# A conditioned two-layer block on one core: the weight deltas' last batch, their loads and their matmuls in another order

## Chip, core and metric

One core of a Trainium2 chip runs the kernel. Its five engines are TensorE (PE: matmuls and transposes; PEld: its weight loads), VectorE (DVE), ScalarE (ACT), GpSimd (POOL) and SyncE (SP, which here issues every DMA). Each works through its own instructions in program order and waits on semaphores for the others. The metric is the device time of one execution in microseconds (us); lower is better. It is given as the median of several runs; one further execution was taken with the profiler.

## What is computed

`x` is 4 batches x 1024 rows x 512, `cond` is 4 x 128 (one row a batch). Two layers follow each other; all is float32 at the interface.

```python
# layer 0
scale = cond @ norm_w.T + 1.0
h = x * (scale[:, None, :] * rsqrt(mean(x * x) + 1e-6))
val, gate = split(h @ up_w.T)                # up_w: 4096 x 512
h = val * gelu(gate)                         # 2048 wide
hq, wq = act_quant(h), weight_quant(down_w)  # 8 bit by row; -1, 0, 1
x = hq @ wq.T + x
# layer 1: its weights depend on the batch
Wd_b = Wd + ((cond @ Wdd.T + bdd) * 0.1).reshape(B, 128, 512)   # Wdd: 65536 x 128
Wu_b = Wu + ((cond @ Wdu.T + bdu) * 0.1).reshape(B, 512, 128)   # Wdu: 65536 x 128
out = x + relu(x @ Wd_b.T + bd) @ Wu_b.T + bu
```

`Wdd` and `Wdu` hold 32 MB each and are read once; every one of their 65536 rows is multiplied with the four rows of `cond`. These products, the *deltas*, are what the change is about.

## The kernel before

**Chunks and slots.** The 4096 rows of x are cut into 8 chunks of 512 (`c` = 0 to 7), and the 2048 columns of h into 16 tiles. Layer 0 runs chunk after chunk, and in each chunk slot after slot (`j` = 0 to 15, one tile a slot); I write (c, j) for a slot. Every engine's program is `chunks(run)`, a loop over the same chunks and slots, so the order of each engine's work is written out by hand. No common clock keeps the engines at the same slot; only semaphores do.

**A slot.** TensorE computes the gate product (12 matmuls of 512 columns, lines 1173 to 1175), ScalarE its gelu (line 693), TensorE the value product (12 more), VectorE the h product of the two (line 1010), ScalarE its absolute value (line 707), VectorE the running maximum (line 902). In the first eight slots of a chunk VectorE and ScalarE also quantise the chunk before (lines 875, 668, 671). In slots 9 to 12 TensorE adds a down product (16 matmuls, line 1277) for 128 rows of the chunk before at the end of the slot; VectorE adds the x rows to it in the slot after (the residual, line 965), and SP stores them and loads the next x rows.

**Deltas on TensorE.** Wdd and half of Wdu are cut into 96 *units* of 128 x 1024 words, each loaded as two halves (`load_nat`, line 382; three buffers `nat`). VectorE turns the two halves of a unit (`turn_nat`, line 892) into `natT`, which has room for four units. Four units make a *batch* (24 batches, m = 0 to 23): `delta_products(m)` (line 1232, 32 small matmuls) waits until all eight halves of the batch are turned and writes into the PSUM bank HY. After every second batch ScalarE copies the bank into `stage` (`read_sums`) and SP stores that to DRAM (`store_stage`).

**The unit table.** `unit_slots` says which units VectorE turns in which slot: one in an ordinary slot, two in slots 9 to 12, none in the slot after a batch's last unit. `batch_at(c, j)` is the batch whose last unit was turned in the slot before (c, j). With this table the 24 delta products stand in the slots (1,1), (1,6), (1,10), (1,13), (2,2), (2,7), (2,11), (2,15), (3,4), (3,9), (3,12), (4,1), (4,6), (4,10), (4,13), (5,2), (5,7), (5,11), (5,15), (6,4), (6,9), (6,12), (7,1) and (7,6).

**Deltas on GpSimd.** The other half of Wdu is cut into 64 *parts*. SP loads a part (`load_part`, line 404), GpSimd multiplies and adds (`multiply_part`, lines 561 to 568), VectorE sums the rest (`sum_part`, line 906). `sum_slots` and `load_slots` say in which slots. A part may only be loaded when GpSimd is nearly through with the part two before it.

**The deltas come back.** In the last chunk, at slot 6, `load_deltas` issues 32 loads from the DRAM scratch into `delta_d` and `delta_u` (the place of `natT`). At slots 10 to 13 TensorE turns one batch of x a slot (`turn_delta_down`, line 1244, and `turn_delta_up`, line 1251), and VectorE adds them to the weights a slot later (`layer_of_batch`). `turn_delta_down(b)` for b > 0 waits for VectorE's work on batch b - 1 of x. After the last chunk comes layer 1, which the change doesn't touch.

**SP's order in a slot** (`run` of SP, line 439 on): x of the next chunk and its turns, weight rows of the units (each waits for the turn of the unit whose buffer it takes), parts, x rows for the residual (`load_xr`, line 409) and their stores, `store_stage`, and at (7,6) `load_deltas`. Everything behind an instruction that waits is issued later too.

TensorE's order in a slot of a later chunk is:

```python
pe.wait_ge(gelu_done, n - 1)
up_products(par, FT + j, GATE[j % 2], gate_full)
...
for m in batch_at(c, j):
    delta_products(m)
if last and 10 <= j < 14:
    turn_delta_down(j - 10)
...
up_products(par, j, VAL[j % 2], val_full)
```

Of the kernel before, what the change touches and what calls it, by code (L numbers as in the profile page):

```python
# [25 lines left out]
def conditioned_block(nc, x, cond, norm_w, up_w, down_w, Wd, bd, Wu, bu, Wdd, bdd, Wdu, bdu, out):  # L26
# [27 lines left out]
    with ExitStack() as ctx:  # L54
# [134 lines left out]
        def first_bank(c, k):  # L189
# [38 lines left out]
        delta_back, delta_turned, layers_ready, layers_hi, layers_split = (sem(n) for n in (  # L228
            "delta_back", "delta_turned", "layers_ready", "layers_hi", "layers_split"))
# [68 lines left out]
        unit_slots, free_from = {}, 13  # L298
        for n in range(FT * NCH):
            long_slot = n >= FT and 9 <= n % FT < 13  # L300
            while free_from <= n and sum(map(len, unit_slots.values())) < UNITS and len(unit_slots.get(n, [])) < 1 + long_slot:
                u = sum(map(len, unit_slots.values()))
                unit_slots.setdefault(n, []).append(u)
                if u % NATT == NATT - 1:
                    free_from = n + 2
# [7 lines left out]
        def batch_of(m):  # L313
# [4 lines left out]
                     for j in ((7, 9, 10, 11, 12, 13, 15) if c == 1 else (1, 3, 5, 7, 8, 9, 10) if c == NCH - 1 else (1, 3, 5, 7, 9, 10, 11, 12, 13, 15))]  # L318
        load_slots = [FT + 3, FT + 3, FT + 6] + [n + 1 for n in sum_slots[:PARTS - 3]]
# [11 lines left out]
        def _(sp):  # L331
# [56 lines left out]
            def load_deltas():  # L388
                sp.wait_ge(stage_free, 16 * (GROUPS + 1))
                sp.wait_ge(nat_turned, 2 * UNITS)  # L390
                for b in range(NB):
                    for k in range(2):
                        n0 = 64 * k
                        sp.dma_start(delta_d[n0:n0 + 32, b, :], delta_of[0][0, b, :, k, 0:4, :]).then_inc(delta_back, 16)
                        for y in range(2):
                            n1 = n0 + 32 + 16 * y
                            sp.dma_start(delta_d[n1:n1 + 16, b, :], delta_of[1][y, b, :, k, 0:4, :]).then_inc(delta_back, 16)
                        sp.dma_start(delta_u[:, 2 * k, b, :], delta_of[0][1, b, :, k, 0:4, :]).then_inc(delta_back, 16)
# [40 lines left out]
            def run(c, par, b):  # L439
                first, last = is_first(c), b is None  # L440
                for j in range(FT):
# [31 lines left out]
                    if c == 1 and j == 3:  # L473
                        sp.wait_ge(piece_quant, FT)
# [9 lines left out]
                    for m in batch_at(c, j):  # L484
                        if m % 2 == 1:
                            store_stage(m)
                    if last and j == 6:
                        load_deltas()
                        sp.wait_ge(x_scaled, TT * NCH - 1)
                        sp.dma_start(bu_bc[:, :], bu.rearrange("(a d) -> a d", a=1).to_broadcast([P, D])).then_inc(bu_in, 16)  # L490
# [48 lines left out]
        def _(pool):  # L539
# [31 lines left out]
            def run(c, par, b):  # L571
# [5 lines left out]
                for i in range(PARTS):  # L577
                    slot = sum_slots[max(i - 2, 0)]
                    if slot // FT == c:
                        if not normed and (i == 1 if c == 1 else slot % FT >= 6):  # L580
                            norm_x(c + 1)
                            normed = True
                        multiply_part(i)
# [554 lines left out]
        def _(pe):  # L1138
# [97 lines left out]
            def turn_delta_down(b):  # L1236
                if b == 0:
                    pe.wait_ge(delta_back, 16 * NB * 8)
# [52 lines left out]
            def run(c, par, b):  # L1291
# [7 lines left out]
                for j in range(FT):  # L1299
# [4 lines left out]
                    if first:  # L1304
                        pe.wait_ge(w_lo_done, halves_done(j, 0))
                    if not (first and j < 2):
                        pe.wait_ge(gelu_done, n - 1)
# [3 lines left out]
                    for m in batch_at(c, j):  # L1311
                        delta_products(m)
# [206 lines left out]
```

## Time and profile before

| | us |
|---|---|
| Median of 3 runs | 947.32 |
| Lowest and highest | 946.69, 947.43 |
| The profiled execution | 946.8 |
| Its span, first to last instruction | 944.6 |
| TensorE busy | 924.6 |
| VectorE busy | 682.3 |
| GpSimd busy | 640.6 |
| ScalarE busy | 428.3 |
| Mean granted clock of TensorE | 0.996 |

The 2.2 us between the profiled execution's time and its span lie outside the first and the last instruction. All times of rows are counted from the start of the span. A timeline row gives start, duration, engine, line of the kernel, operation, output and input; where the engine stood idle before it, the idle time and what ended it stand in brackets. TensorE's matmuls are pipelined: a matmul of 512 columns is shown as 0.38 us long while the next begins 0.22 us after it, so slots are measured from start to start. Chunk c's slots are found in the timeline by the h products of VectorE (line 1010), of which there is one a slot.

### The profile page before, as it was taken

Reading aid. Unit: us, or ns where it says so; the run is one execution under the profiler, and the core shown is the slowest. Engines: PE = TensorE matmul, PEld = TensorE weight load, DVE = VectorE, ACT = ScalarE, POOL = GpSimd, SP = SyncE. Lnnn points to the kernel's source line nnn. Section 1 sums busy time; section 2 is a strip of 40 time slices with the busy share of each in tenths; the row PEclk is TensorE's granted clock in tenths of the full one; section 3 lists DMA queues with packets and bytes.
Section 4 is the critical chain, followed back from the end, with each engine's and each line's share of the span. In section 5 each row is a group of like instructions: output and inputs, shape, how many; then the busy total and the mean of one; then the engine's idle time right before and its main releaser. Section 6 shows DMA issues by size and latency. Waiting matters only on the chain. (4 is left out here: it accounts for less than half of the span.)

```text
span 944.6 us, 13871 instructions
## 1 busy us (share of the span) xinstructions
PE 924.6 (98%) x5002; PEld 454.2 (48%) x5002; DVE 682.3 (72%) x1034; ACT 428.3 (45%) x788; POOL 640.6 (68%) x565
## 2 busy tenths in 40 slices
PE   9999999999999999999999999999999999599998
PEld 6555544444444444444444444444444444245586
DVE  6778877877877588767878687777877694156666
ACT  7898676224731276225632275224722264014343
POOL 1000009989987999799987899799988997300664
PEclk9999999999999999999999999999999999989999
DMA  8799644565255454564355553563446451221584
GB/s 293 240 218 216 171 140 130 142 191 164 82 151 157 127 168 130 142 162 136 111 157 161 129 166 111 153 184 111 124 131 185 131 179 56 79 67 35 189 301 178
DMA packets 142059, 144.04 MB, mean 152 GB/s; under 512 B 51876, under 2 KB 89256, under 8 KB 141480
## 3 DMA queue, kind: packets, MB, share of 16 engines
q1 hardware_dynamic: 141992, 143.17, 52.0%
q8 instruction: 39, 0.64, 0.3%
q14 instruction: 28, 0.23, 0.1%
HBM read 112.46 MB, written 19.92 MB: 140 GB/s over the span
## 5 line engine op out<-in xcount | busy, mean ns | idle before, releaser
L561 POOL TENSOR_TENSOR delta_reg<-delta_reg,s_bc 128x512 f32<-128x512 f32 x256 | 327.2, 1299 | 153.3 <-DMA delta_reg<-in_L_cond_Wdu 141.9
L1173 PE MATMUL bank<-x_split,w_hi 128*128 128x512 f16 x1016 | 386.5, 380 | 0.0
L1174 PE MATMUL bank<-x_split,w_hi 128*128 128x512 f16 x1016 | 386.1, 380 | 0.0
L1175 PE MATMUL bank<-x_split,w_lo 128*128 128x512 f16 x1016 | 386.1, 380 | 0.0
L892 DVE STREAM_TRANSPOSE delta_reg<-delta_reg 128x512 f32<-128x512 f32 x192 | 198.7, 1117 | 17.6 <-DMA delta_reg<-in_L_cond_Wdd 13.9
L707 ACT ACTIVATE bank<-h 128x512 f32<-128x512 f32 x126 | 75.7, 601 | 292.7 <-DVE h L1010 292.5
L1010 DVE SCALAR_TENSOR_TENSOR h<-bank,desc,g 128x512 f32<-128x512 f32 x128 | 95.2, 743 | 110.5 <-issue 89.3
L564 POOL TENSOR_TENSOR delta_reg<-delta_reg 128x512 f32<-128x512 f32 x128 | 166.9, 1304 | 10.0
L1173 PEld LDWEIGHTS bank<-x_split,w_hi 128*128 128x128 f16 x1016 | 99.6, 98 | 122.1 <-issue 10.7
L1175 PEld LDWEIGHTS bank<-x_split,w_lo 128*128 128x128 f16 x1016 | 99.6, 98 | 120.5 <-issue 1.1
L1174 PEld LDWEIGHTS bank<-x_split,w_hi 128*128 128x128 f16 x1016 | 99.6, 98 | 112.7 <-issue 0.8
L693 ACT ACTIVATE g<-bank,desc 128x512 f32<-128x512 f32 x128 | 87.3, 682 | 115.1 <-PE bank L1175 114.9
L568 POOL TENSOR_TENSOR delta_reg<-delta_reg 128x256 f32<-128x256 f32 x128 | 96.0, 750 | 12.9 <-DVE delta_reg L906 3.1
L1277 PE MATMUL bank<-wqT,qreg 128*128 128x512 fp8e4 x448 | 101.3, 379 | 1.4 <-DVE xr L965 1.4
L902 DVE TENSOR_TENSOR absrun<-bank,absrun 128x512 f32<-128x512 f32 x118 | 81.2, 688 | 21.4 <-ACT bank L707 21.4
L668 ACT ACTIVATE h<-h 128x512 f32<-128x512 f32 x112 | 64.7, 623 | 36.6 <-DVE h L875 36.6
L875 DVE TENSOR_TENSOR h<-h,bank 128x512 f32<-128x512 f32 x112 | 71.6, 683 | 0.0
L1277 PEld LDWEIGHTS bank<-wqT,qreg 128*128 128x128 bf16 x448 | 43.7, 98 | 53.8 <-DVE xr L965 1.6
L671 ACT ACTIVATE qreg<-h 128x512 bf16<-128x512 f32 x112 | 63.6, 616 | 0.0
L965 DVE SCALAR_TENSOR_TENSOR xr<-bank,fy,xr 128x512 f32<-128x512 f32 x30 | 22.3, 745 | 40.4 <-issue 19.1
L604 POOL TENSOR_TENSOR out_own<-xn,sc_row 128x512 f32<-128x512 f32 x8 | 10.1, 1287 | 58.9 <-DVE h L1117 56.3
L906 DVE TENSOR_REDUCE delta_reg<-delta_reg 128x16 f32<-128x512 f32 x64 | 41.8, 652 | 10.2 <-POOL delta_reg L568 10.2
(182 smaller groups left out, 754.7 us busy)
## 6 DMA issues: line engine op xcount, KB each, us to landing
delta_reg<-in_L_cond_Wdd SPq DMA_DIRECT2D x128, 256.0 KB, 2.9
delta_reg<-in_L_cond_Wdu SPq DMA_DIRECT2D x128, 256.0 KB, 3.2
qreg<-in_L_cond_up_w SPq DMA_DIRECT2D x32, 256.0 KB, 4.4
xr<-in_x SPq DMA_DIRECT2D x30, 256.0 KB, 3.9
x_scratch<-xr SPq DMA_DIRECT2D x30, 256.0 KB, 3.5
xn<-in_x SPq DMA_DIRECT2D x7, 1024.0 KB, 7.5
h<-in_L_cond_down_w SPq DMA_DIRECT2D x4, 1024.0 KB, 6.8
delta_reg<-in_L_cond_down_w SPq DMA_DIRECT2D x8, 512.0 KB, 4.6
```

The lines of the kernel that those rows point to most:

```text
L561: pool.tensor_tensor(part_mul[:, b, :, :], part_w[:, i % 2, :, :], cond_all[:, 2 * pair + b, :].unsqueeze(1).to_broadcast([P, 4, C]), ALU. ...
L564: pool.tensor_tensor(part_mul[:, :, :, 0:64], part_mul[:, :, :, 0:64], part_mul[:, :, :, 64:128], ALU.add).then_inc(part_step, 1)
L568: pool.tensor_tensor(part_low[:, i % 2, 2 * pair:2 * pair + 2, :, :], part_mul[:, :, :, 0:32], part_mul[:, :, :, 32:64], ALU.add).then_inc ...
L693: act.activation(g[:, j % 2, :], GATE[j % 2][:, :], ACT.Gelu, scale=desc[:, 2 * j + 1:2 * j + 2]).then_inc(gelu_done, 1)
L707: act.activation(abs_tile(c, j), h[:, j, :], ACT.Abs).then_inc(abs_done, 1)
L892: dve.transpose(natT[:, t, k, :, :].rearrange("p a (r e) -> p e a r", e=4), nat[:, v % HALVES, :]).then_inc(nat_turned, 1)
L902: dve.tensor_tensor(absrun[:, :], abs_tile(c, j), absrun[:, :], ALU.max).then_inc(max_done, 1)
L1010: dve.scalar_tensor_tensor(h[:, j, :], VAL[j % 2][:, :], desc[:, 2 * j:2 * j + 1], g[:, j % 2, :], ALU.mult, ALU.mult).then_inc(h_done, 1)
L1173: pe.matmul(bank[:, :], w_hi[:, k, cols], xh[:, par, k, :], start=(k == 0), stop=False)
L1174: pe.matmul(bank[:, :], w_hi[:, k, cols], xl[:, par, k, :], start=False, stop=False)
L1175: mm = pe.matmul(bank[:, :], w_lo[:, k, cols], xh[:, par, k, :], start=False, stop=(k == KD - 1))
L1277: mm = pe.matmul(Y[:, :], q[:, f, t * P:(t + 1) * P], wqT[:, f, :], start=(f == 0), stop=(f == FT - 1))
```

## The change

It has four parts.

1. The unit table is built in another way. After a batch's last unit the next slot now turns one unit fewer than usual (none in an ordinary slot, one in slots 9 to 12), where it turned none before in either. From chunk 3 on every chunk has the same pattern. The 24 delta products now stand in the slots (1,1), (1,6), (1,10), (1,13), (2,2), (2,7), (2,11), (2,14), and then 3, 8, 11 and 14 of chunks 3, 4, 5 and 6. None is left in chunk 7.
2. GpSimd's parts are loaded and summed sooner: the first three loads two slots sooner, the sums of chunk 1 begin at slot 5 and not 7, one sum fewer stands in chunk 7, and a part's load stands in a slot of a sum and not in the slot after it. GpSimd's `norm_x(2)` now comes before part 3, where it came before part 1.
3. `load_deltas` loads one batch of x a call, at slots 1 to 4 of chunk 7, and has a semaphore for each batch of x; `turn_delta_down(b)` waits for its own.
4. TensorE's `delta_products` stands ahead of the gate product of its slot and not behind it.

```diff
-        unit_slots, free_from = {}, 13
-        for n in range(FT * NCH):
+        unit_slots, units, batch_end = {}, 0, -1
+        for n in range(FT - 3, FT * NCH):
             long_slot = n >= FT and 9 <= n % FT < 13
-            while free_from <= n and sum(map(len, unit_slots.values())) < UNITS and len(unit_slots.get(n, [])) < 1 + long_slot:
-                u = sum(map(len, unit_slots.values()))
-                unit_slots.setdefault(n, []).append(u)
-                if u % NATT == NATT - 1:
-                    free_from = n + 2
+            for _ in range(1 + long_slot - (batch_end == n - 1)):
+                if units < UNITS and batch_end != n:
+                    unit_slots.setdefault(n, []).append(units)
+                    units += 1
+                    if units % NATT == 0:
+                        batch_end = n
...
-                     for j in ((7, 9, 10, 11, 12, 13, 15) if c == 1 else (1, 3, 5, 7, 8, 9, 10) if c == NCH - 1 else (1, 3, 5, 7, 9, 10, 11, 12, 13, 15))]
-        load_slots = [FT + 3, FT + 3, FT + 6] + [n + 1 for n in sum_slots[:PARTS - 3]]
+                     for j in ((5, 7, 9, 10, 11, 12, 13, 15) if c == 1 else (1, 3, 5, 7, 9, 10) if c == NCH - 1 else (1, 3, 5, 7, 9, 10, 11, 12, 13, 15))]
+        load_slots = [FT + 1, FT + 1, FT + 4] + sum_slots[:PARTS - 3]
...
-            def load_deltas():
-                sp.wait_ge(stage_free, 16 * (GROUPS + 1))
-                sp.wait_ge(nat_turned, 2 * UNITS)
-                for b in range(NB):
-                    for k in range(2):
...
+            def load_deltas(b):
+                if b == 0:
+                    sp.wait_ge(stage_free, 16 * (GROUPS + 1))
+                    sp.wait_ge(nat_turned, 2 * UNITS)
+                for k in range(2):
...
-                    if c == 1 and j == 3:
-                        sp.wait_ge(piece_quant, FT)
+                    if c == 1 and j == 1:
+                        sp.wait_ge(piece_quant, FT - 2)
...
+                    if last and 1 <= j <= NB:
+                        load_deltas(j - 1)
                     if last and j == 6:
-                        load_deltas()
...
-                        if not normed and (i == 1 if c == 1 else slot % FT >= 6):
+                        if not normed and slot % FT >= 6:
...
             def turn_delta_down(b):
+                pe.wait_ge(delta_back[b], 16 * 8)
                 if b == 0:
-                    pe.wait_ge(delta_back, 16 * NB * 8)
...
+                    for m in batch_at(c, j):
+                        delta_products(m)
                     if not (first and j < 2):
                         pe.wait_ge(gelu_done, n - 1)
                     up_products(par, FT + j, GATE[j % 2], gate_full)
                     if not first and j == 0:
                         turn_absrun(c - 1)
-                    for m in batch_at(c, j):
-                        delta_products(m)
```

## Rows read from the trace of the kernel before

**Rows 1.** The page: busy time of the engines; granted clock in 40 slices.
```profile
PE 924.6 (98%) x5002; PEld 454.2 (48%) x5002; DVE 682.3 (72%) x1034; ACT 428.3 (45%) x788; POOL 640.6 (68%) x565
...
PEclk9999999999999999999999999999999999989999
```

**Rows 2.** Waits of PE: line, releaser: total us, times, longest.
```profile
PE bank L1232 <- DVE delta_reg L892: 1.9, 3, 0.6
```

**Rows 3.** Timeline of PE, chunk 7: start, us, engine, line, operation [idle <-releaser].
```profile
804.49 0.38 PE L1173 MATMUL bank<-x_split,w_hi 128*128 128x512 f16 x1
...
809.50 0.66 PE L1244 MATMUL bank<-identf,delta_reg 128*128 128x128 f32 x4 [2.26 <-DMA delta_reg<-delta_scratch]
...
814.38 3.63 PE L1277 MATMUL bank<-wqT,qreg 128*128 128x512 fp8e4 x16 [1.41 <-DVE xr L965]
...
827.70 1.12 PE L1244 MATMUL bank<-identf,delta_reg 128*128 128x128 f32 x4 [7.11 <-DVE wd_first L921]
...
836.97 0.38 PE L1173 MATMUL bank<-x_split,w_hi 128*128 128x512 f16 x1
...
846.25 0.38 PE L1173 MATMUL bank<-x_split,w_hi 128*128 128x512 f16 x1
...
852.09 0.38 PE L1173 MATMUL bank<-x_split,w_hi 128*128 128x512 f16 x1
```

**Rows 4.** Timeline of SP's queue, chunk 7.
```profile
789.73 0.34 SPq L394 DMA_DIRECT2D delta_reg<-delta_scratch  x1
...
808.47 0.43 SPq L409 DMA_DIRECT2D xr<-in_x  x1
```

**Rows 5.** Timeline of DVE, chunk 7, slot 10.
```profile
813.57 0.75 DVE L965 SCALAR_TENSOR_TENSOR xr<-bank,fy,xr 128x512 f32<-128x512 f32 x1 [10.17 <-DMA xr<-in_x]
823.69 0.69 DVE L906 TENSOR_REDUCE delta_reg<-delta_reg 128x16 f32<-128x512 f32 x1 [9.37 <-POOL delta_reg L568]
```

**Rows 6.** Timeline of PE, early slots of chunks 1, 2 and 3.
```profile
117.50 0.38 PE L1173 MATMUL bank<-x_split,w_hi 128*128 128x512 f16 x1
...
120.89 1.93 PE L1232 MATMUL bank<-delta_reg,cond_diag 128*32 128x256 f32 x32 [0.64 <-DVE delta_reg L892]
...
229.97 0.38 PE L1173 MATMUL bank<-x_split,w_hi 128*128 128x512 f16 x1
...
233.32 1.93 PE L1232 MATMUL bank<-delta_reg,cond_diag 128*32 128x256 f32 x32 [0.60 <-DVE delta_reg L892]
...
336.09 0.38 PE L1173 MATMUL bank<-x_split,w_hi 128*128 128x512 f16 x1
...
341.27 0.38 PE L1173 MATMUL bank<-x_split,w_hi 128*128 128x512 f16 x1
```

**Rows 7.** Timeline of DVE, chunks 2, 3 and 5.
```profile
233.66 0.73 DVE L1010 SCALAR_TENSOR_TENSOR h<-bank,desc,g 128x512 f32<-128x512 f32 x1
...
257.52 2.07 DVE L892 STREAM_TRANSPOSE delta_reg<-delta_reg 128x512 f32<-128x512 f32 x2
...
312.43 2.06 DVE L892 STREAM_TRANSPOSE delta_reg<-delta_reg 128x512 f32<-128x512 f32 x2
...
339.28 0.78 DVE L1010 SCALAR_TENSOR_TENSOR h<-bank,desc,g 128x512 f32<-128x512 f32 x1
...
341.73 2.10 DVE L892 STREAM_TRANSPOSE delta_reg<-delta_reg 128x512 f32<-128x512 f32 x2
343.64 0.70 DVE L1010 SCALAR_TENSOR_TENSOR h<-bank,desc,g 128x512 f32<-128x512 f32 x1
...
627.26 2.06 DVE L892 STREAM_TRANSPOSE delta_reg<-delta_reg 128x512 f32<-128x512 f32 x2
```

**Rows 8.** Timeline of PE, starts of slots (2,7), (2,14) and (5,14).
```profile
258.51 0.38 PE L1173 MATMUL bank<-x_split,w_hi 128*128 128x512 f16 x1
...
312.53 0.38 PE L1173 MATMUL bank<-x_split,w_hi 128*128 128x512 f16 x1
...
628.51 0.38 PE L1173 MATMUL bank<-x_split,w_hi 128*128 128x512 f16 x1
```

More of the change, by code:

```diff
@@ L227, in conditioned_block @@
             "nat_turned", "delta_mm", "stage_full", "stage_free"))
-        delta_back, delta_turned, layers_ready, layers_hi, layers_split = (sem(n) for n in (
-            "delta_back", "delta_turned", "layers_ready", "layers_hi", "layers_split"))
+        delta_back = [sem(f"delta_back{b}") for b in range(NB)]
+        delta_turned, layers_ready, layers_hi, layers_split = (sem(n) for n in (
+            "delta_turned", "layers_ready", "layers_hi", "layers_split"))
         xr_in = [sem(f"xr_in{i}") for i in range(2)]
@@ L386, in store_stage @@
                 sp.dma_start(delta_dram[m // 2, :, :], stage[:, :]).then_inc(stage_free, 16)
-            def load_deltas():
-                sp.wait_ge(stage_free, 16 * (GROUPS + 1))
-                sp.wait_ge(nat_turned, 2 * UNITS)
-                for b in range(NB):
-                    for k in range(2):
[L393 to L398, printed above, removed]
+            def load_deltas(b):
[3 more added lines that the diff above has]
+                for k in range(2):
+                    n0 = 64 * k
+                    sp.dma_start(delta_d[n0:n0 + 32, b, :], delta_of[0][0, b, :, k, 0:4, :]).then_inc(delta_back[b], 16)
+                    for y in range(2):
+                        n1 = n0 + 32 + 16 * y
+                        sp.dma_start(delta_d[n1:n1 + 16, b, :], delta_of[1][y, b, :, k, 0:4, :]).then_inc(delta_back[b], 16)
+                    sp.dma_start(delta_u[:, 2 * k, b, :], delta_of[0][1, b, :, k, 0:4, :]).then_inc(delta_back[b], 16)
             def load_part(i):
```

## The prediction

> **What bounds the kernel now.** I read the page first. TensorE is busy for 924.6 of 944.6 us, the others for at most 682.3 [rows 1], so only two things can move the time: an interval in which TensorE stands idle or runs at the lower clock, and work added to it. The change adds none; it moves work. The question is therefore where TensorE waits, and where it will wait.
>
> The timeline of TensorE has one bad place, the last chunk's slots 10 and 11: it waits 2.26, 1.41 and 7.11 us [rows 3], 10.8 us together. The clock digits are 9 in every slice but one, and that slice (826 to 850 us) begins within the 7.11 us stall [rows 1]. The chain behind it is read on the issuing queue. SP issues the 32 loads of the summed deltas in one piece (and bu's behind them), from 789.73 until the x rows' own at 808.47 [rows 4]: 18.7 us in which the x rows, and Wdu part 63 right behind them, stand in the queue. VectorE then waits 10.17 us for the x rows and 9.37 us for GpSimd's sums of part 63, and gets to them at 823.69 [rows 5]; TensorE's 7.11 us is the end of that chain.
>
> Everywhere else in chunks 1 to 7 TensorE waits three times, for 1.9 us together, for VectorE's transposes ahead of a delta product [rows 2]. They are small, but they say that this wait is already tight where the product stands today, behind a gate product.
>
> **The change part by part.**
>
> *Deltas loaded a batch a slot, last batch a chunk sooner.* From the unit table: the last delta product moves from (chunk 7, slot 6) to (6,14), so the stage is stored before chunk 7 and the loads can go at (7,1) to (7,4), eight each. 18.7 us for 32 issues is 4.7 us for eight, against 5.18 us for a plain slot (336.09 to 341.27 [rows 6]), and SP has no weight rows to load there any more. Part 63 is asked for at slot 5 and x rows at slot 7, behind no block of loads. All three stalls lose their cause. The gain is best read as lengths: slot 10's start to slot 14's start took 852.09 − 804.49 = 47.6 us; slots 12 and 13 of the same kind, undisturbed, took 9.28 and 5.84 [rows 3]; three of the first and one of the second are 33.7. **Gain 13.9 us**, of which 10.8 is idle and 3.1 the slow clock and restarts. What is late next there: turning batch b+1's delta waits for VectorE's batch b; in slots 12 and 13 that was already so and cost nothing [rows 3]. The extra per-batch waits on TensorE are met six slots ahead: nothing.
>
> *Parts a slot sooner, GpSimd's first norm behind part 2.* GpSimd is below TensorE in busy time [rows 1] and gets its first part two slots sooner, so it is further ahead. SP's wait for GpSimd at an earlier slot is the risk: the loads queued behind it are x rows and the next weight rows. The norm is wanted at (1,8) and comes about (1,7). I charge nothing; the cover is GpSimd's head start of two slots, some 10 us.
>
> *Delta products ahead of the gate product.* 24 products of the same cost, so no added work. But TensorE runs in order, and `delta_products(m)` waits for the batch's eight transposes, of which the last two are VectorE's in the slot before. Today a gate product (12 matmuls, 2.6 us) lies between; now nothing does. If VectorE is late by the end of a slot, TensorE stands, and nothing later gives it back, as it waits for nothing else in these chunks. Queued behind the wait are gate, value and down products, that is everything. So I take the 24 batches by their new slot and compare the end of the last transposes with the start of that slot.
>
> - (1,1), batch 0. TensorE's slot began at 117.50, the product could begin at 120.89 [rows 6]. It now waits 3.4 us instead of 0.64: 2.75 more.
> - (2,2), batch 4. 229.97 and 233.32 [rows 6], 3.35 instead of 0.60: 2.75 more. The third old wait (0.6, [rows 2], batch 15 at (5,2)) goes, as that batch moves.
> - (3,3), (4,3), (5,3), (6,3). Batches now end in slot 2 of each of these chunks, where VectorE still works off what chunk start piled up. In chunk 3 slot 2's transposes ended at 341.73 + 2.10 = 343.83, TensorE's slot 3 began at 341.27 [rows 6, 7]: 2.6 us. That chunk had no unit in slot 15 before it; the new table has one there, as chunk 2 had. In chunk 2 VectorE's h product (line 1010) of slot 1 came 233.66 − 229.97 = 3.7 us after TensorE's slot 2 start, in chunk 3 it came 339.28 − 336.09 = 3.2 [rows 6, 7]: 0.5 later. So 2.6 to 3.1; I take 3.0, the chunk with the same units in slots 15 to 1: 12.0 us for four.
> - (2,7). Slot 6 holds the mean square: transposes to 257.52 + 2.07 = 259.59, slot 7 from 258.51 [rows 7, 8]: 1.1.
> - (3,8) to (6,8), four. One slot after that; VectorE gains 0.8 a slot (343.64 − 339.28 = 4.4 against 5.18, [rows 6, 7]): 0.25 each, 1.0. Bounds 0 and 1.1 each.
> - (2,14) to (6,14), five. In slot 13 the transposes stand behind the residual of x rows 3, whose load SP issues behind slot 12's four weight loads. With the same units in slots 12 and 13, chunk 2 ended them at 312.43 + 2.06 = 314.49 against a slot 14 start of 312.53, chunk 5 at 629.32 against 628.51 [rows 7, 8]: 2.0 and 0.8. Five at 1.4: 7.0. Bounds: 0, if the x rows land in time, and 2.0 each.
> - The other eight, in (1,6), (1,10), (1,13) and slot 11: a down product of 3.4 us (9.28 − 5.84, [rows 3]) or a TensorE already late by batch 0 lies between: 0.
>
> Sum: 2.75 + 2.75 − 0.6 + 12.0 + 1.1 + 1.0 + 7.0 = **26.0 us lost**, against 13.9 gained: +12.1. The profiled execution took 946.8 us (span 944.6), so 958.9; the median of the runs is 0.5 above it, so **959 us**.
>
> With all lower ends (5.5 − 0.6 + 10.4, nothing at slots 7, 8 and 14): 15.3 lost, +1.4, 948.7. With all upper ends (5.5 − 0.6 + 12.4 + 1.1 + 4.4 + 10.0): 32.8 lost, +18.9, 966.2.
>
> **The rivals.**
>
> *Clock.* The new waits at slot 3, (1,1) and (2,2) are idle gaps of about 3 us, six of them. Gaps of 2.26 and 1.41 left the clock at full, 7.11 was followed by the lower level [rows 1, 3], and 3 lies nearer to the first. If each of the six were followed by a slow stretch like that one's, it would cost up to 3.1 each, 18.6 in all: 978; three of six, 969. For it: it has happened once here. Against: TensorE is fully busy on both sides of each gap. Chance 0.10.
> The Trainium skill, page "TensorE: Matmul & The Clock Gate", section "Why this matters for your kernels", advises to leave no long idle gap between bursts of matmuls, or the clock drops to the lower level. The 7.11 us stall agrees; by that rule read strictly the six gaps make this rival, and by the two short gaps they don't.
>
> *Faster.* Only (1,1), (2,2) and (2,7) cost what I say, and the waits of slots 3 and 14 do not come, because SP's loads leave sooner and VectorE is never behind. Then 5.5 − 0.6 + 1.1 = 6.0 is lost and 946.8 − 13.9 + 6.0 = 939. It decides at 13.9 − 6.0 = 7.9 us for these nine places, 0.9 each: below that the change wins. For it: slot 14's wait hangs on when one load lands, and ranged from 0.8 to 2.0. Against: in slot 2 VectorE's operations follow each other without idle time [rows 7], so no earlier load makes it sooner. Chance 0.13.
>
> *The last chunk isn't cured.* Part 63 or the x rows still come late, because SP now waits for GpSimd at earlier slots and the delta loads queue behind that. Then the 13.9 is not there and the 26.0 is: 973. Against: by its new place part 63 is asked for five slots ahead of its sum. Chance 0.04.
>
> **How the numbers follow.** The forecast's own cases run from 949 to 966 with 0.68, and its low end down to no change with 0.05; the clock has 0.10, no cure 0.04, faster 0.13. Within 0.2% (1.9 us, about what a measurement of this kernel can tell from no change) is 945.4 to 949.2. So slower 0.82, same 0.05, faster 0.13. The range that leaves out the faster case and the upper part of the clock and no-cure cases is 948 to 972.
>
> **What would show it.** In the new trace: SP's delta loads at chunk 7's slots 1 to 4, no stall of TensorE in its slots 10 and 11 and a full clock to the end (the gain); waits of line `delta_products` for VectorE's transposes, in place of 3 of 0.6 us, some 15 with 20 to 27 us in total, the longest near 3 us at the start of slot 3 of chunks 3 to 6 (the loss). I am wrong if those waits total less than 14 us, if they are there but TensorE later finds the time again, or if a clock digit of chunks 1 to 6 falls below 9.

## The result: 3.5% slower, nearly three times as far from before as forecast

| | before | changed |
|---|---|---|
| median of the runs | 947.01 us (946.10 to 947.43, 4 runs) | 980.71 us (977.31 to 982.90, 4 runs) |
| ratio to before | 1 | 1.0354, 95% interval 1.0323 to 1.0385 |
| profiled execution, its span | 946.8, 944.6 us | 982.9, 980.7 us |
| mean granted clock of TensorE | 0.996 | 0.987 |

The forecast was 959 us with a range of 948 to 972; the sign was right, the size was not: 33.7 us slower by the medians where 12 were forecast. The profiled execution is the slowest of the four and has the lowest clock; the other three had 0.991 to 0.993, so what is said of the low clock below is the upper end of what it cost. The page of the changed kernel, busy time and granted clock, to be laid beside [rows 1]:

```profile
PE 933.5 (95%) x5002; PEld 455.6 (46%) x5002; DVE 695.5 (71%) x1034; ACT 429.0 (44%) x788; POOL 645.0 (66%) x565
...
PEclk9999999999999999999899999999999999999999
```

The same 5002 matmuls keep TensorE busy for 8.9 us more; the rows below show where they ran at the lower clock. A digit below 9 now stands in the middle of the kernel (466 to 490 us), not in the last chunk. TensorE's waits (line, releaser: total us, times, longest), against the 1.9 us in 3 of [rows 2]; line 1235 is the delta product, line 895 VectorE's transposes of the weight rows:

```profile
PE bank L1235 <- DVE delta_reg L895: 38.4, 20, 4.0
```

Some 15 waits with 20 to 27 us were forecast. TensorE's timeline shows four of the twenty, and what stands behind some of them:

```profile
267.19 1.93 PE L1235 MATMUL bank<-delta_reg,cond_diag 128*32 128x256 f32 x32 [2.01 <-DVE delta_reg L895]
...
413.80 1.93 PE L1235 MATMUL bank<-delta_reg,cond_diag 128*32 128x256 f32 x32 [0.95 <-DVE delta_reg L895]
...
472.45 3.64 PE L1235 MATMUL bank<-delta_reg,cond_diag 128*32 128x256 f32 x32 [3.97 <-DVE delta_reg L895]
476.02 0.61 PE L1176 MATMUL bank<-x_split,w_hi 128*128 128x512 f16 x1
476.42 0.63 PE L1177 MATMUL bank<-x_split,w_hi 128*128 128x512 f16 x1
...
556.08 3.60 PE L1235 MATMUL bank<-delta_reg,cond_diag 128*32 128x256 f32 x32 [2.01 <-DVE delta_reg L895]
559.62 0.39 PE L1176 MATMUL bank<-x_split,w_hi 128*128 128x512 f16 x1
```

The number behind the start is the duration: the same 32 matmuls take 1.93 us at 267 and 3.6 us at 472 and 556, and at 476 the gate product's matmuls take 0.61 in place of 0.38 us. These are stretches at the lower of the clock's two levels. Beside [rows 3], the last chunk's slots 10 to 14 in TensorE's timeline (a product of line 1176 at each slot's start):

```profile
854.53 0.38 PE L1176 MATMUL bank<-x_split,w_hi 128*128 128x512 f16 x1
...
863.82 0.38 PE L1176 MATMUL bank<-x_split,w_hi 128*128 128x512 f16 x1
...
873.11 0.38 PE L1176 MATMUL bank<-x_split,w_hi 128*128 128x512 f16 x1
...
888.23 0.38 PE L1176 MATMUL bank<-x_split,w_hi 128*128 128x512 f16 x1
```

No stall is left there, slots 10 and 11 take 9.29 us each, and slot 10 to slot 14 takes 33.7 us against 47.6. SP's queue, beside [rows 4], now spreads the loads; part 63 goes out at 824.80 between them and the x rows:

```profile
804.41 0.44 SPq L396 DMA_DIRECT2D delta_reg<-delta_scratch  x1
...
824.80 0.59 SPq L406 DMA_DIRECT2D delta_reg<-in_L_cond_Wdu  x1
825.44 0.50 SPq L493 DMA_DIRECT2D sc_row<-in_L_cond_bu  x1
825.98 0.92 SPq L411 DMA_DIRECT2D xr<-in_x  x2
```

**The balance of the 36.1 us** between the two profiled executions: 38.4 − 1.9 = 36.5 of waits, minus 13.9 in the last chunk, is 22.6. The low clock adds 10.4: a delta product's start to the next gate product's takes 1.87 us at full clock and 3.20, 3.47, 3.04, 3.57, 3.54 and 2.89 behind six of the waits (8.5 us more together), and in three of them the twelve gate matmuls take 2.85, 3.15 and 3.00 in place of 2.38 (1.9 more). That makes 33.0. Of the remaining 3.1, waits of TensorE that the kernel before doesn't have take 1.5 (for the scales `s` 0.7, `absmax` 0.5, x rows 0.3); 1.6 I can't assign to a row.

### The profile page after: what moved, and what is told of

Read it like the earlier page. It is cut to its first block, busy times and chain, and to the rows that moved or that the text cites. A ratio compares the mean times of both kernels' runs of the same rounds, so it can differ in the third digit from the quotient of the medians.

```text
span 980.7 us, 13874 instructions
## 1 busy us (share of the span) xinstructions
PE 933.5 (95%) x5002; PEld 455.6 (46%) x5002; DVE 695.5 (71%) x1034; ACT 429.0 (44%) x788; POOL 645.0 (66%) x565
## 4 chain that ended last, share of the span: by engine, by line
PE 77%; DVE 8%; DMA 5%; issue 3%; POOL 3%; ACT 2%; SPq 1%; DVEq 0%; POOLq 0%; ACTq 0%
PE bank L1176 19%; PE bank L1177 19%; PE bank L1178 19%; PE bank L1280 6%; PE bank L1235 5%; DVE delta_reg L895 4%; DMA delta_reg<-in_L_cond_Wdd 4%; POOL delta_reg L564 1%; PE bank L1290 1%; DVE absrun L905 1%; POOL delta_reg L567 1%; PE bank L1417 1%; PE bank L1426 1%; PE bank L1156 1%; PE bank L1447 1%
## 5 line engine op out<-in xcount | busy, mean ns | idle before, releaser
L564 POOL TENSOR_TENSOR delta_reg<-delta_reg,s_bc 128x512 f32<-128x512 f32 x256 | 331.8, 1317 | 90.7 <-DMA delta_reg<-in_L_cond_Wdu 77.7
L895 DVE STREAM_TRANSPOSE delta_reg<-delta_reg 128x512 f32<-128x512 f32 x192 | 196.7, 1107 | 20.7 <-DMA delta_reg<-in_L_cond_Wdd 17.2
L1176 PEld LDWEIGHTS bank<-x_split,w_hi 128*128 128x128 f16 x1016 | 99.6, 98 | 124.2 <-issue 12.6
L571 POOL TENSOR_TENSOR delta_reg<-delta_reg 128x256 f32<-128x256 f32 x128 | 94.8, 741 | 92.1 <-DVE delta_reg L909 83.6
L1235 PE MATMUL bank<-delta_reg,cond_diag 128*32 128x256 f32 x768 | 54.9, 435 | 38.4 <-DVE delta_reg L895 38.4
L1235 PEld LDWEIGHTS bank<-delta_reg,cond_diag 128*32 128x32 f32 x768 | 24.9, 122 | 66.3 <-DVE delta_reg L895 48.8
```

The lines of the kernel that those rows point to most:

```text
L564: pool.tensor_tensor(part_mul[:, b, :, :], part_w[:, i % 2, :, :], cond_all[:, 2 * pair + b, :].unsqueeze(1).to_broadcast([P, 4, C]), ALU. ...
L571: pool.tensor_tensor(part_low[:, i % 2, 2 * pair:2 * pair + 2, :, :], part_mul[:, :, :, 0:32], part_mul[:, :, :, 32:64], ALU.add).then_inc ...
L895: dve.transpose(natT[:, t, k, :, :].rearrange("p a (r e) -> p e a r", e=4), nat[:, v % HALVES, :]).then_inc(nat_turned, 1)
L1176: pe.matmul(bank[:, :], w_hi[:, k, cols], xh[:, par, k, :], start=(k == 0), stop=False)
L1235: mm = pe.matmul(HY[32 * t:32 * t + 32, cols], cond_diag[:, a, :], natT[:, (4 * m + t) % NATT, :, a, :], start=(a == 0), stop=(a == HB - 1))
```

## The experiments

My theory A: moving the delta products ahead of the gate product costs it all, in waits and in the low clock behind them, and the other parts of the change gain about what the last chunk lost. Rival B: the other parts lose time too. In the table, the waits for transposes are TensorE's in the profiled execution, and the clock is its mean granted clock there. Each run was timed against the kernel before on the same chip: 945.19 us beside the runs e1, e2, e7 and e8, 946.21 beside e3 to e6, 946.24 beside e9, e12 and e13; intervals are of 95%.

| run | median, us | ratio (interval) | waits for transposes | clock |
|---|---|---|---|---|
| e1_behind_gate | 939.21 | 0.9931 (0.9914 to 0.9947) | 4.6 us in 8 | 0.999 |
| e2_order_alone | 973.47 | 1.0296 (1.0281 to 1.0312) | 22.6 in 12 | 0.989 |
| e3_old_parts | 972.98 | 1.0293 (1.0248 to 1.0338) | 31.9 in 18 | 0.984 |
| e4_units_and_loads | 940.08 | 0.9940 (0.9920 to 0.9960) | 4.1 in 7 | 0.999 |
| e5_parts_alone | 936.77 | 0.9904 (0.9888 to 0.9921) | 1.8 in 3 | 1.000 |
| e6_behind_value | 937.48 | 0.9913 (0.9892 to 0.9933) | none | 1.000 |
| e7_filled | 975.62 | 1.0317 (1.0300 to 1.0334) | 21.8 in 19 | 0.995 |
| e8_turn_first | 960.32 | 1.0147 (1.0118 to 1.0176) | 17.6 in 16 | 0.998 |
| e9_value_turn_first | 946.02 | 1.0013 (0.9988 to 1.0039) | none | 0.997 |
| e12_batchwise_loads | 934.84 | 0.9889 (0.9871 to 0.9907) | 3.6 in 4 | 1.000 |
| e13_batchwise_behind_value | 934.50 | 0.9876 (0.9858 to 0.9894) | none | 1.000 |

### The order of the delta products, undone and alone

**e1_behind_gate**, the changed kernel with the product back behind the gate product:

```diff
-                    for m in batch_at(c, j):
-                        delta_products(m)
                     if not (first and j < 2):
                         pe.wait_ge(gelu_done, n - 1)
                     up_products(par, FT + j, GATE[j % 2], gate_full)
                     if not first and j == 0:
                         turn_absrun(c - 1)
+                    for m in batch_at(c, j):
+                        delta_products(m)
```

> The changed kernel with one part undone: TensorE's delta products stand behind the gate product again. Theory A (the loss is TensorE waiting at a slot's start for transposes of the slot before, and the low clock that follows): the gate product's 2.6 us come off each wait, of the changed kernel's 38.4 us in 20 waits some 4 us stay, the slow stretches (10 us) go, the last chunk's gain of 13.9 us stays: 947.0 - 13.9 + 2 = 935 us. Theory B (the loss comes from the denser unit table and the parts' new slots, which make VectorE, GpSimd and SP late wherever the product stands): most of the 33.7 us stays, above 965 us.

**e2_order_alone**, the kernel before with only this move made, the other way round.

> The kernel before with one part of the change alone: TensorE's delta products ahead of the gate product. Theory A: waits of 3.4 us at (1,1), (2,2), (5,2), 1.3 at (4,1), 1.7 and 1.9 at (3,4) and (6,4), some 1 us at (2,7), (5,7), (2,15), 0.7 at (1,13), (4,13) and (7,1), by the ends of the transposes in the trace of before: 19 us more than before's 1.9, and 2 to 5 us of low clock, none of the last chunk's gain: 947.0 + 19 + 4 = 970 us. Theory B: the old table's waits stay small, under 952 us.

Measured 939.21 and 973.47. Together they show that the move is the loss: taking it out of the changed kernel brings 4.2% of the time (1.0354 against 0.9931, some 40 us), putting it alone into the kernel before costs 3.0%, 28.3 us. Of these, the waits for transposes are 20.7 and the low clock 6.2 (by the same reckoning as above, behind four of the waits). The same move costs some 12 us more on the new table and slots, where the transposes come later: it adds 33.8 us of waits to e1's 4.6, and 20.7 to the 1.9 of the kernel before. In e1 the waits of TensorE are these, the first with 4.6 us where the changed kernel has 38.4, and the last chunk's slots 10 to 14 again take 33.7 us:

```profile
PE bank L1235 <- DVE delta_reg L895: 4.6, 8, 1.5
...
PE bank L1176 <- DVE absrun L905: 0.9, 1, 0.9
PE bank L1280 <- DVE xr L968: 0.8, 1, 0.8
```

The second half of theory A, that the other parts gain what the last chunk lost, holds only in part: e1 came out 4 us above what A expected. With 13.9 gained, 6.0 (by the medians) is what is left. Waits that grew by 2.7, 0.9 and 0.8 account for 4.4 of the missing 7.9; the rest is not assigned.

### The other parts of the change, one by one

**e5_parts_alone**, the kernel before with only the parts' new slots, the earlier wait of SP and the norm's new place:

```diff
-((7, 9, 10, 11, 12, 13, 15) if c == 1 else (1, 3, 5, 7, 8, 9, 10) if c == NCH - 1 else ...
-        load_slots = [FT + 3, FT + 3, FT + 6] + [n + 1 for n in sum_slots[:PARTS - 3]]
+((5, 7, 9, 10, 11, 12, 13, 15) if c == 1 else (1, 3, 5, 7, 9, 10) if c == NCH - 1 else ...
+        load_slots = [FT + 1, FT + 1, FT + 4] + sum_slots[:PARTS - 3]
...
-                        if not normed and (i == 1 if c == 1 else slot % FT >= 6):
+                        if not normed and slot % FT >= 6:
```

> The kernel before with the parts' slots and GpSimd's norm changed alone. The prediction charged nothing: 945.2 us as before, within 1.5. Rival 1 (the last chunk's stalls shrink by themselves, as part 63 is asked for ahead of the 32 loads): the second of the two waits of VectorE (9.4 us) goes, TensorE's 7.1 us stall with it, 936 to 940 us. Rival 2 (SP waits for GpSimd ahead of x rows): 947 to 950 us.

Measured 936.77: the first rival. The prediction had charged and credited nothing here. Yet these few numbers take away the 7.11 us stall and its slow clock by themselves. In e5's SP queue part 63 leaves well ahead of the block of delta loads, which still stands in one piece; in TensorE's timeline of the last chunk two small stalls are left of three:

```profile
773.21 0.43 SPq L404 DMA_DIRECT2D delta_reg<-in_L_cond_Wdu  x1
790.76 0.34 SPq L394 DMA_DIRECT2D delta_reg<-delta_scratch  x1
...
809.23 0.91 SPq L409 DMA_DIRECT2D xr<-in_x  x2
```

```profile
810.17 0.66 PE L1244 MATMUL bank<-identf,delta_reg 128*128 128x128 f32 x4 [1.90 <-DMA delta_reg<-delta_scratch]
...
814.20 3.63 PE L1277 MATMUL bank<-wqT,qreg 128*128 128x512 fp8e4 x16 [0.56 <-DVE xr L965]
```

The x rows are loaded no sooner than in [rows 4]. So of the two things that stood behind the block, part 63 was the one that made the long stall.

**e4_units_and_loads**, the kernel before with the new unit table and the loads a batch a slot (parts 1 and 3 of the change), old slots of the parts, product behind the gate product.

> The kernel before with the unit table and the loads of the deltas alone (parts and order of the product as before). Theory A: as the run with the product behind the gate, 939.2 us, since a product behind the gate hides what the parts' slots cost at slot 8; with theory D some of its waits shrink: 937 to 940 us. Rival (the parts' shift is needed for the last chunk's gain): part 63 late again, above 943 us.

Measured 940.08. The two gains don't add up: each change cures the long stall alone (6.1 us faster here, 9.4 in e5), and both together are e1, 6.0 us faster. The unit table brings waits of its own, in e4 in its waits of TensorE for the transposes (4.1 us), the spread of the scales and the residual of the x rows:

```profile
PE bank L1235 <- DVE delta_reg L895: 4.1, 7, 1.5
PE bank L1270 <- DVE s L870: 2.7, 5, 0.8
PE bank L1280 <- DVE xr L968: 2.3, 3, 1.4
```

**e3_old_parts**, the changed kernel with the parts' slots, SP's wait and the norm as before (the diff of e5 turned round).

> The changed kernel with part 2 undone: GpSimd's parts loaded and summed in the slots of the kernel before, the first norm ahead of part 1. Theory D: the parts' new slots lay a GpSimd operation over VectorE's mean-square operation in slot 6 (it takes 1.24 us there, 0.17 us in most chunks of before), and that is why the waits at (2,7) and slot 8 are 2.0 and 0.7 to 1.1 us and not 1.1 and 0.25: they fall by 0.9 us on average, five of them, 980.7 - 4.5 = 976 us. Rival: the waits of these slots are the table's: 980.7 us. Nothing of either says that the 13.9 us of the last chunk go.

Measured 972.98. The interval is wide and overlaps that of the changed kernel (1.0248 to 1.0338, 1.0323 to 1.0385), so the time decides little and the trace has to: the waits for transposes fell from 38.4 to 31.9 us. At slot 8 of chunks 3 to 6 they are 0, 0, 0 and 0.22 in place of 0.71 to 1.11, and at (2,7) 0.95 in place of 2.01, as the prediction had them. At slot 14 they fell too, from 9.8 to 6.0 us over the five; at slot 3 they rose, from 12.6 to 13.9. The reason at slot 8 and (2,7) is in VectorE's timeline in slot 6, where a small operation, the mean square of line 842, lies just ahead of the transposes. The changed kernel, then GpSimd's work at that time, then e3:

```profile
378.90 1.24 DVE L842 TENSOR_SCALAR ss<-ss 128x4 f32<-128x4 f32 x1 [1.31 <-ACT x_split L619]
```

```profile
377.62 2.50 POOL L564 TENSOR_TENSOR delta_reg<-delta_reg,s_bc 128x512 f32<-128x512 f32 x2
```

```profile
379.23 0.17 DVE L842 TENSOR_SCALAR ss<-ss 128x4 f32<-128x4 f32 x1 [1.31 <-ACT x_split L619]
```

It takes 1.24 to 1.27 us in six of the seven times that the changed kernel runs it, and ends with an operation of GpSimd, here the second of two (377.62 + 2.50 = 380.12; 378.90 + 1.24 = 380.14). In e3 it takes 0.17 to 0.45, in the kernel before 0.17 to 0.83 in six of seven. What differs is the moment: in e3 GpSimd's operation is nearly through when the mean square begins, in the changed kernel it has just begun, at most 0.06 us before. GpSimd there waits for VectorE 21 times, 83.6 us in all (3.1 in 3 in the kernel before), and I take this to tie the two to the same place of each chunk:

```profile
POOL delta_reg L571 <- DVE delta_reg L909: 83.6, 21, 7.7
```

The old slots don't keep the two apart by themselves: e4 has them, and its mean square takes 0.58 to 1.06 us in five of seven. e3 undoes all of part 2 at once, so it doesn't tell the parts' slots from SP's wait and the norm.

The Trainium skill, page "SBUF — State Buffer", section "SBUF: two separate sides", says that GpSimd and a VectorE operation of some kinds (in a mode with two ports, or with two inputs in SBUF) hold a shared pair of ports for a whole instruction while the other waits. The ends that coincide agree with it; no run here shows the port itself, or the mode of this operation.

### How late the transposes are, and behind what

**e6_behind_value**, the changed kernel with the product behind the value product, not only behind the gate product:

```diff
                     up_products(par, j, VAL[j % 2], val_full)
+                    for m in batch_at(c, j):
+                        delta_products(m)
```

> The changed kernel with TensorE's delta products at the end of the two products of a slot, behind the value product (5.2 us later than the change has them). Theory A: every wait for transposes is covered (the longest was 4.0 us), so the 5.6 us that the product behind the gate still lost go: 939.2 - 5.6 = 934 us, the fastest of all. Rival (VectorE waits for the product before it may turn the next unit, since four units fill its buffer): the lateness comes back on VectorE in slots 9 and 12, 939 us or more.

Measured 937.48: no wait for a transpose is left. VectorE's lateness is thus nowhere over some 5 us, two products' time. The time is 3.5 us above what was expected. The expected 5.6 us counted 1.0 more than e1 waits for transposes (4.6), and beside e1 the waits for the x rows grew from 0.8 to 2.4 and those for the running maximum from 0.9 to 1.1; 0.7 stays open. The two in e6:

```profile
PE bank L1280 <- DVE xr L968: 2.4, 4, 0.7
...
PE bank L1176 <- DVE absrun L905: 1.1, 1, 1.1
```

**e8_turn_first**, the changed kernel with VectorE's transposes ahead of the quantising and the running maximum in slots 1 to 7. If slot 3's wait is VectorE's queue and not a late load, it must shrink.

```diff
+                    if not first and 0 < j < 8:
+                        turn_units(c, j)
...
-                    if j > 0 and not first:
+                    if j >= 8 and not first:
```

> The changed kernel, and in slots 1 to 7 of every later chunk VectorE turns its units ahead of the quantising and the running maximum, not behind them. Theory A (the waits at slots 3 and 8 are VectorE's own backlog, so its order inside the slot sets them): the last transposes end 1.9 us sooner, waits at (3,3) to (6,3) fall from 3.1 to 1.2 us on average, those at slot 8 and (2,7) go, the clock stays full at slot 3: about -13 us of waits and -5 of slow clock, 962 us. Rival (the weight rows come late, SP's loads set the waits): VectorE would only wait for the rows instead, 978 to 983 us.

Measured 960.32. VectorE's timeline of the changed kernel ahead of slot 3 shows what stood in front, without idle time, and below it is the product in e8, with 0.46 us where 2.88 stood:

```profile
353.66 1.27 DVE L878 TENSOR_TENSOR h<-h,bank 128x512 f32<-128x512 f32 x2
354.85 0.68 DVE L905 TENSOR_TENSOR absrun<-bank,absrun 128x512 f32<-128x512 f32 x1
355.45 2.02 DVE L895 STREAM_TRANSPOSE delta_reg<-delta_reg 128x512 f32<-128x512 f32 x2
```

```profile
351.66 1.93 PE L1237 MATMUL bank<-delta_reg,cond_diag 128*32 128x256 f32 x32 [0.46 <-DVE delta_reg L895]
```

Slot 8's waits went to zero too, and only (1,1), 3.20 us, was still followed by the low clock. But new waits of 4.1 us for the running maximum came: VectorE's order moves the lateness from one result to another.

**e9_value_turn_first**, both: behind the value product, and the transposes first in slots 2 to 7.

> The changed kernel with its delta products behind the value product and with VectorE turning the weight rows ahead of its other work in slots 2 to 7. With the products behind the value product alone TensorE had no wait for transposes left and the time was 937.5 on the same chip as 946.2 for the kernel before. If the time hung on these transposes only, turning them first can bring nothing: 937 to 938. If VectorE's other results (quantised pieces, maxima) come later for it and TensorE waits for them as it did where turning first stood with the product ahead of the gate product (4.1 us in 4 waits there), it is 939 to 942.

Measured 946.02, the median of nine runs (942.48 to 952.97); a tenth took 3446.9 us, which nothing here explains, and is left out. It is worse than both readings: with the transposes no longer awaited, turning them first only delays the rest. In e9 TensorE waits, where e6 had 1.1 and 2.4 us,

```profile
PE bank L1178 <- DVE absrun L905: 7.1, 3, 3.6
PE bank L1282 <- DVE xr L968: 3.1, 5, 1.0
```

### The slow clock behind the gaps

**e7_filled**, the changed kernel with idle matmuls on a free bank ahead of the delta product, 40 of them at (2,2) and at slot 3, 18 at slot 14. They compute nothing that is used.

```diff
+                        if (c, j) == (2, 2) or (c > 1 and j in (3, 14)):
+                            keep_busy({14: 18}.get(j, 40), TA)
                     for m in batch_at(c, j):
                         delta_products(m)
```

> The changed kernel with matmuls of no use in the gaps: 40 of 128 columns (some 2.5 us) ahead of the delta product at (2,2) and in slot 3 of chunks 3 to 6, 18 (some 1.1 us) in slot 14 of chunks 2 to 7's table, into a bank that is free there. Theory C (part of the loss is the clock, which falls after gaps of 2.8 us and more): the six slow stretches go, waits for the transposes shrink by what the fill takes, the sum of both stays: 980.7 - 10 = 971 us, mean clock back to 0.996 or more. Rival: the low clock isn't made by these gaps: no change, 981 us, or some us more where the fill is longer than the gap.

Measured 975.62, ratio 1.0317 (1.0300 to 1.0334) against 1.0354 (1.0323 to 1.0385), so the time alone doesn't show a gain: the intervals overlap. In e7's timeline of TensorE the fillers take 2.40 us and the product at slot 3 of chunk 3 its 1.93 at full clock; unfilled (1,1) is now followed by the low clock:

```profile
122.24 3.64 PE L1235 MATMUL bank<-delta_reg,cond_diag 128*32 128x256 f32 x32 [3.44 <-DVE delta_reg L895]
...
355.70 2.40 PE L1296 MATMUL bank<-identb 128*128 128x128 bf16 x40
359.83 1.93 PE L1235 MATMUL bank<-delta_reg,cond_diag 128*32 128x256 f32 x32 [1.73 <-DVE delta_reg L895]
```

All ten filled places kept the full clock, where six had lost it. The lateness itself didn't change: 21.8 us of waits and 17.4 of fillers (5 times 2.40, 5 times 18 at 0.06) are 39.2, against 38.4. Two unfilled gaps, (1,1) and (2,7), then cost 2.6 and 1.6 us of low clock, so that 6.2 of the 10.4 us came back and not all. The mean clocks of all runs say the same: 0.995 to 1.000 in the four of e7, 0.987 to 0.993 in the four of the changed kernel. That the gaps cause the low clock is shown. The bound of 2.8 us that theory C gives them is not: in the changed kernel's own trace 3.19, 3.17 and 2.87 us stand at (1,1), (2,2) and (6,3), of which only the second was followed by it, and 2.01 us at (4,14) was.

### Towards a faster kernel

**e12_batchwise_loads**, e5 with the loads of the summed deltas a batch a slot at slots 6 to 9 of the last chunk, x rows and bu between, and the old unit table:

```diff
-                    if last and j == 6:
-                        load_deltas()
+                    if last and 6 <= j < 6 + NB:
+                        load_deltas(j - 6)
+                    if last and j == 6 + NB - 1:
                         sp.wait_ge(x_scaled, TT * NCH - 1)
```

> The kernel before, with the new slots of the parts (as in the run that changed them alone) and with the summed deltas' loads issued a batch of x a slot, at slots 6 to 9 of the last chunk, each batch with a semaphore of its own; the unit table is the old one and the delta products stay behind the gate product. If the 1.90 us stall on the delta loads and the 0.57 us on the x rows, left over in the last chunk with the parts' slots alone (936.8 against 946.2), come from SP's one block of 32 issues, both shrink below 0.5 us together and the time is 934 to 935, 0.988 of before. If they come from when the last batch's deltas reach memory, the 1.90 us stays and the time is 936.5 to 937.5, 0.990.

**e13_batchwise_behind_value**, that with the delta product behind the value product.

> The run before (parts' slots, loads a batch a slot, old unit table) with the delta products behind the value product in place of behind the gate product, so 5 us instead of 2.6 us after the slot begins. The three waits of 0.6 us for VectorE's transposes in chunks 1 to 5 go, and no other wait takes their place, as the stage and the down product that follow have slack: 1.9 us less than the run before, 932 to 934, 0.986 of before. If the later product pushes GpSimd's or VectorE's work on the bank's contents out, new waits of about 1 us come and the time is that of the run before or above it, 935 to 937.

Measured 934.84 and 934.50: 1.1 and 1.2% below the kernel before, and the two fastest medians of this study, though e5's interval (0.9888 to 0.9921) overlaps both. The two stalls that e5 had left in the last chunk are gone, as the first reading had it, though a new wait for transposes of 1.71 us stands at 785 us in e12. Between the two kernels there is no difference that the intervals can tell, where 1.9 us was expected: in e13 the waits for transposes are gone, 3.6 us, but those for the running maximum and the scales rose from 0.9 and 0.4 to 1.8 and 1.4:

```profile
PE bank L1175 <- DVE absrun L904: 1.8, 1, 1.8
PE bank L1269 <- DVE s L869: 1.4, 3, 0.6
```

## Why the prediction missed, step by step

Two steps failed. The waits were put at 27.9 us and measured 38.4; and the low clock behind them was put at nothing, on the ground that 3 us lies nearer to 2.26 than to 7.11, and cost 10.4. The prediction's own sign of being wrong, a clock digit below 9 in chunks 1 to 6, is there.

**What held.** The last chunk's gain was 13.9 us, to the tenth. The delta product's move was the loss, by the mechanism described. (1,1) and (2,2) waited 3.19 and 3.17 us (3.4 and 3.35 forecast), the four slots 3 2.88, 3.97, 2.89 and 2.87, together 12.6 (12.0 forecast). The faster rival fell with them.

**Where the waits were mis-sized.** 27.9 us of idle was forecast (26.0 and the old 1.9), 38.4 came, above the 34.7 of all upper ends together. e3 has 31.9: 6.5 of the 10.6 us too many go with part 2, the parts, for which the prediction charged nothing.

- "The other eight: 0" was wrong for the four at slot 11: 0.95, 1.04, 1.00 and 0.99, 4.0 us. The step said that a down product of 3.4 us lies between. It does (3.63 us, at 409.22), but VectorE is later than that: slots 9 and 10 each turn two units, and in them it waits for weight rows, in the changed kernel's timeline of VectorE:

```profile
403.23 1.09 DVE L895 STREAM_TRANSPOSE delta_reg<-delta_reg 128x512 f32<-128x512 f32 x1 [2.24 <-DMA delta_reg<-in_L_cond_Wdd]
...
412.65 1.10 DVE L895 STREAM_TRANSPOSE delta_reg<-delta_reg 128x512 f32<-128x512 f32 x1 [0.63 <-DMA delta_reg<-in_L_cond_Wdd]
```

  I had counted what covers the wait without asking how late its end is, and had read no row of a slot with two units. That the load's wait causes it is read from these rows, not tried.
- Slot 8 was 3.7 us and not 1.0, and (2,7) 2.0 and not 1.1. In e3 what was too much is gone in both, with the mean square's 1.1 us under GpSimd's operations. The step "parts a slot sooner: I charge nothing" looked at SP's and GpSimd's own order only, and not at what GpSimd's operations do to VectorE's beside them.
- Slot 14, five times, was 9.8 us and not 7.0, with (2,14) at 2.85 above the bound of 2.0. The transposes stand behind the residual of slot 13, as the prediction had it, and VectorE's timeline of the changed kernel shows this residual late:

```profile
321.41 0.75 DVE L968 SCALAR_TENSOR_TENSOR xr<-bank,fy,xr 128x512 f32<-128x512 f32 x1 [4.29 <-issue]
322.07 1.99 DVE L895 STREAM_TRANSPOSE delta_reg<-delta_reg 128x512 f32<-128x512 f32 x2
```

  The idle time ahead of it was 3.67 us in the kernel before. What ended it the row doesn't tell. The bounds came from two old chunks with the old slots of the parts; with these slots, in e3, (2,14) is 1.33 and the five are 6.0, inside the bounds.

**The clock.** This was the rival with 0.10, and it came in good part: six stretches, 10.4 us. It had priced a stretch at up to 3.1 us; in the runs one cost 1.3 to 2.9. My argument against, that gaps of 2.26 and 1.41 us left the clock at full and 3 lies nearer to them than to 7.11, had two points below and one above, and placed the boundary by distance, which no row supported. That TensorE is fully busy on both sides of a gap, the other argument, held and did not help. I also counted only the six gaps near 3 us, and two of the low stretches came at slot 14.

**What this adds to.** Slot 11 4.0, slot 8 2.7, slot 14 2.8, (2,7) 0.9 and slot 3 0.6, less 0.4 at (1,1) and (2,2), are 10.6 more waiting; the clock is 10.4 more; 3.1 is the rest of the balance above. That is the 24.0 us between 958.9 and 982.9. With the waits alone it would have been 969.5, still inside the range. The range missed since I had added no case in which waits and clock come out high together, though one begets the other.

**A right number for a wrong reason.** The 13.9 us was laid to the loads a batch a slot and the earlier last batch. e5 shows that the parts' slots alone get 9.4 us of gain, so that the change had two cures for one stall, and needed only one, the cheaper.

## What to carry to other kernels

When a step that waits is moved forward in an in-order queue, list for each place how late its input is, not only what used to lie between, and read that from the busiest slot and from the slot with the most transfers. In this kernel a gap of 2 us and more in TensorE's work has to be priced at up to twice its length, for the slow clock that can follow it (2.9 us behind one of 2.9 in e3). And when a stall has two things behind one block, move each alone first: here one small edit (the parts' slots, 9.4 us) was worth more than all parts together.

## What the runs showed of the hardware

**The low clock and the length of a gap.** In the changed kernel, e2, e3, e7 and e8, TensorE's waits ahead of delta products of 2.75 us or more were followed by the low clock 17 times of 20, waits of 1.89 to 2.02 us 2 times of 6, and none shorter. A gap of 3.19 us at 121 us of the changed kernel was not followed by it, one of 2.01 at 556 was. The length alone doesn't decide; what else does stays open. The Trainium skill, page "TensorE: Matmul & The Clock Gate", section "Why this matters for your kernels", bids to leave no long idle gaps between bursts of matmuls; the 17 of 20 agree. With small matmuls of 128x128 ahead of the wait (60 ns each) the clock stayed up in all ten places of e7; what idle time was left there was 1.73 us at most.

**A small operation of VectorE under GpSimd's.** The mean square, 128x4 elements, took 0.17 us with nothing of GpSimd beside it (at 50.36 us of the changed kernel). Where an operation of GpSimd was running when it began, it ended within 0.04 us of that operation's end: after 1.24 to 1.27 us in the changed kernel, where that had just begun, 0.58 to 1.06 in e4 and 0.20 to 0.45 in three of e3's, where less of it was left. Where less than 0.17 was left it took its own 0.17. Where both began together (255.65 us of the kernel before) it took 0.17.
